# Narrow attentions: products with values in a bank of their own, in pieces, and turned tiles in three banks

## The reference

```python
q = (queries @ q_w + q_b)            # 16 heads of width 16
k, v = (keys @ k_w + k_b), (keys @ v_w + v_b)
scores = einsum('bhqd,bhkd->bhqk', q, k) * scale   # masked
attn = softmax(scores)
out = einsum('bhqk,bhkd->bqhd', attn, v) @ out_w + out_b
```

## Time and profile before

| | |
|---|---|
| median of 3 runs | 1073.18 us (1072.58 to 1073.34) |
| the profiled execution's own time | 1071.5 us |
| its span, first to last instruction | 1069.7 us |
| mean granted TensorE clock | 0.947 of full speed |
| busy: PE, DVE, ACT, POOL | 945.1, 777.2, 606.4, 312.2 us |
| loop of L0a, 32 heads | from 45 to about 162 us |
| loop of L2a | from 831 to about 911 us |
| loop of L3a | from 945 to about 1024 us |

### The profile page before, as it was taken

The page is one execution under the profiler, slowest core; times in us unless marked ns, Lnnn a source line. Parts: engine busy times, 40 slices in busy tenths (PEclk is TensorE's granted clock), DMA queues, the critical chain, the costliest instruction groups (busy, mean ns, idle before and its releaser), DMA issues. The chain is left out here.

```text
span 1069.7 us, 17955 instructions
## 1 busy us (share of the span) xinstructions
PE 945.1 (88%) x6616; PEld 802.0 (75%) x6616; DVE 777.2 (73%) x1621; ACT 606.4 (57%) x1375; POOL 312.2 (29%) x321
## 2 busy tenths in 40 slices
PE   4789886889999999999799999999596898779958
PEld 4666665778999999998689989898475566656647
DVE  3486766468878888886688988878664688668864
ACT  3587883236565555554455655456534688267842
POOL 3454550050221222221121132200004456445510
PEclk8899997989999999999999999999888699889989
DMA  4996004140110111110210111000206820394020
GB/s 144 266 238 103 2 1 185 67 164 1 41 40 1 40 41 40 41 40 2 79 41 3 39 40 41 1 1 2 78 7 159 208 46 2 101 245 67 1 85 21
DMA packets 39506, 72.71 MB, mean 68 GB/s; under 512 B 6550, under 2 KB 23960, under 8 KB 37244
## 3 DMA queue, kind: packets, MB, share of 16 engines
q1 hardware_dynamic: 39420, 71.56, 25.0%
HBM read 55.28 MB, written 16.27 MB: 67 GB/s over the span
## 5 line engine op out<-in xcount | busy, mean ns | idle before, releaser
L1356 ACT CAST L1a_probsT_hi<-L1a_bank 128x512 fp32r<-128x512 f32 x128 | 69.0, 589 | 85.0 <-PE L1a_bank L1232 84.9
L1180 POOL TENSOR_SCALAR L1a_wo_hi<-L1a_stage 128x512 fp32r<-128x512 f32 x16 | 10.4, 652 | 347.5 <-PE L1a_sums L74 339.7
L1391 ACT ACTIVATE L1a_probs<-L1a_scores,L1a_neg_max 128x512 f32<-128x512 f32 x128 | 86.9, 684 | 33.7 <-DVE L1a_bias_shifted L1516 29.2
L1512 DVE TENSOR_REDUCE L1a_top<-L1a_scores 128x2 f32<-128x1024 f32 x64 | 78.2, 1223 | 18.1 <-PE L1a_scores L74 18.1
L72 PE MATMUL L1a_bank<-L1a_probsT_hi,L1a_v_hi 128*128 128x256 f32 x256 | 73.5, 287 | 10.4 <-DVE L1a_probsT_lo L1427 10.4
L1427 DVE TENSOR_TENSOR L1a_probsT_lo<-L1a_bank,L1a_probsT_hi 128x512 fp32r<-128x512 f32 x128 | 82.0, 682 | 0.1
L1358 ACT ACTIVATE L1a_attended_hi<-L1a_bank,L1a_cols 128x256 fp32r<-128x256 f32 x64 | 30.5, 477 | 83.7 <-PE L1a_bank L74 83.5
L72 PE MATMUL L1a_bank<-L1a_w_hi,ctxT_hi 128*128 128x256 f32 x256 | 74.8, 292 | 0.0
L417 POOL TENSOR_SCALAR L0a_probs<-L0a_probs,L0a_inverse 128x768 f32<-128x768 f32 x64 | 57.2, 906 | 58.7 <-DVE L0a_inverse L686 58.7
L74 PE MATMUL L1a_bank<-L1a_probsT_hi,L1a_v_lo 128*128 128x256 f32 x256 | 72.8, 284 | 0.0
L73 PE MATMUL L1a_bank<-L1a_probsT_lo,L1a_v_hi 128*128 128x256 f32 x256 | 72.8, 284 | 0.0
(11 more groups left out here) (422 smaller groups left out, 3089.1 us busy)
## 6 DMA issues: line engine op xcount, KB each, us to landing
L1a_stage<-in_L_w SPq DMA_DIRECT2D x15, 1024.0 KB, 4.8
L0m_fold_wq<-in_L_wqT SPq DMA_DIRECT2D x2, 2048.0 KB, 12.9
L0a_k_dram<-L0a_kT_hi SPq DMA_DIRECT2D x8, 384.0 KB, 10.6
L0a_k_stack<-L0a_k_dram SPq DMA_DIRECT2D x4, 576.0 KB
L0a_w_qkv<-L0a_k_dram SPq DMA_DIRECT2D x4, 576.0 KB
L0a_wide_wo<-in_L_wo SPq DMA_DIRECT2D x1, 2048.0 KB, 17.3
L0a_wide_wo<-in_L_wo SPq DMA_DIRECT2D x2, 1024.0 KB, 18.2
L0m_stage<-in_L_wm SPq DMA_DIRECT2D x4, 512.0 KB, 6.1
```

The costliest lines, as they stand in the source:

```text
L1356: nc.scalar.copy(out, source).then_inc(ring.hi_done, 1)
L1391: nc.scalar.activation(probs[:, g % 2, qt, :], scores[:, qt, :], ACT.Exp, bias=neg_max[:, g % 2, qt:qt + 1], accum_out=row_sum[:, g % 2, q ...
L1512: link(nc.vector.tensor_reduce(top[:, :], scores[:, :, :], AX.X, ALU.max))
```

## The change

The ring loses a bank: one of the four is taken out of it and holds the products with values of all units, one after the other, with semaphores of its own (`values_full`, `values_high`, `values_done`). The turned tiles rotate in the three that are left, and so do all other jobs. A product is cut along the keys into PIECES (3 with 512 keys, with 1, 1 and 2 of the 4 key tiles; 2 with 768 keys, with 3 of the 6 key tiles each), and piece i of unit u stands ahead of the turn of t = 4u + 5 + i. `high_v` and `low_v` come in the step of the last piece, and on ACT and DVE behind that step's copies. On ACT the copy of the first turned bank (c = 0) moves between the two exponentials of a step. The first piece of a unit waits for `low_v` of the unit before, and so does the last unit's product, which is in one. The bias values become two jobs, behind the turns of t = 14 and 15. The turned probabilities get 4 + PIECES slots in place of 5.

```diff
-        TSLOTS = 5
+        PIECES = 3 if nk == S else 2
+        TSLOTS = 4 + PIECES
...
+        values_bank = banks.pop()
         ring = ph.ring(banks)
+        values_full, values_high, values_done = ph.sem("values_full"), ph.sem("values_high"), ph.sem("values_done")
...
-        def product_before(t):
-            return t // 4 - 1 if t % 4 == 1 and t >= 4 else None
-        BIAS_UNIT = 2
+        def piece_beside(t):
+            return divmod(t - 5, 4) if t >= 5 and (t - 5) % 4 < PIECES else None
+        def last_piece(t):
+            return piece_beside(t) is not None and piece_beside(t)[1] == PIECES - 1
+        def bias_beside(t):
+            return t - 14 if cfg["bias_values"] and t in (14, 15) else None
+        values = values_bank[:, 0:Q]
...
-            def product_v(unit):
-                job = job_of["V", unit, 0]
-                ring.wait_bank(pe, job)
+            def product_v(unit, first=0, end=PIECES):
                 b, quad = divmod(unit, quads)
-                for back in range(ring.n):
-                    ring.wait_evacuated(pe, unit_copies(unit)[-1 - back])
-                for kt in range(nkt):
+                if first == 0:
+                    if unit:
+                        pe.wait_ge(values_done, unit)
+                    for back in range(ring.n):
+                        ring.wait_evacuated(pe, unit_copies(unit)[-1 - back])
+                for kt in range(first * nkt // PIECES, end * nkt // PIECES):
...
-                last.then_inc(ring.full, 1)
+                if end == PIECES:
+                    last.then_inc(values_full, 1)
...
                 if t >= 0:
-                    if product_before(t) is not None:
-                        product_v(product_before(t))
-                        if cfg["bias_values"] and product_before(t) == BIAS_UNIT:
-                            values_of_bias()
+                    if piece_beside(t) is not None:
+                        unit, piece = piece_beside(t)
+                        product_v(unit, piece, piece + 1)
                     transpose_head(t)
+                    if bias_beside(t) is not None:
+                        values_of_bias(bias_beside(t))
...
+            def copy_turned(t, c):
+                job = job_of["T", t, c]
+                act.wait_ge(ring.full, job + 1)
+                nc.scalar.copy(probsT[:, t % TSLOTS, c * 512:(c + 1) * 512],
+                               ring.bank(job)[:, :]).then_inc(ring.freed_by(job), 1)
+
             def evacuate(t):
-                if product_before(t) is not None:
-                    high_v(product_before(t))
...
-                for c in range(tj):
+                for c in range(1, tj):
                     if by_act(t, c):
+                        copy_turned(t, c)
+                if last_piece(t):
+                    high_v(piece_beside(t)[0])
...
             for g in range(HEADS + LAG):
                 if g < HEADS:
                     for m in (2 * g, 2 * g + 1):
+                        if m % 2 and g >= LAG:
+                            copy_turned(g - LAG, 0)
                         small = m % small_slots
                         act.wait_ge(max_done, m + 1)
...
+                elif g >= LAG:
+                    copy_turned(g - LAG, 0)
                 if g >= LAG:
                     evacuate(g - LAG)
...
                 if t >= 0:
-                    if product_before(t) is not None:
-                        low_v(product_before(t))
                     for c in range(tj):
                         if not by_act(t, c):
...
+                    if last_piece(t):
+                        low_v(piece_beside(t)[0])
```

More of the change, by code:

```diff
@@ L452, in _, with values_of_bias @@
                 last.then_inc(ring.full, 1)
-            def values_of_bias():
-                job = job_of["B", 0, 0]
+            def values_of_bias(i):
+                job = job_of["B", i, 0]
                 pe.wait_ge(spread_ready, 1)
@@ L458, in values_of_bias @@
                 ring.wait_bank(pe, job)
[L459 to L464, removed]
+                for c in range(4):
+                    for j in range(4):
+                        h = 4 * j + c
+                        last = nc.tensor.matmul(ring.bank(job)[32 * j:32 * j + 32, 0:D], spread[:, i, h, :],
+                                                wide_wo(i * H + h), start=c == 0, stop=c == 3)
                 last.then_inc(ring.full, 1)
@@ L487, in product_v @@
                         moving = probsT[:, g % TSLOTS, :].rearrange("p (t k n) -> p t k n", t=2, k=nkt)[:, :, kt, :]
-                        last = nc.tensor.matmul(ring.bank(job)[32 * j:32 * j + 32, 0:Q],
+                        last = nc.tensor.matmul(values[32 * j:32 * j + 32, :],
                                                 v[:, b * nkt + kt, 32 * (4 * quad + j):32 * (4 * quad + j) + 32],
                                                 moving, start=kt == 0, stop=kt == nkt - 1)
-                last.then_inc(ring.full, 1)
+                if end == PIECES:
+                    last.then_inc(values_full, 1)
             for g in range(HEADS + LAG):
@@ L520, in _ @@
                 if t == 0:
-                    ring.wait_evacuated(pe, job_of["V", own, 0])
+                    pe.wait_ge(values_done, own + 1)
                 if t == 2:
-                    ring.wait_evacuated(pe, job_of["V", own - 1, 0])
+                    pe.wait_ge(values_done, own)
                 ring.wait_bank(pe, job)
@@ L570, in _ @@
                 last.then_inc(ring.freed_by(job), 1)
-            def evacuate(t):
-                if product_before(t) is not None:
-                    high_v(product_before(t))
[L576 to L580, removed]
-                for c in range(tj):
-                    if by_act(t, c):
[L583 to L587, removed]
+            def copy_turned(t, c):
[3 more added lines that the diff above has]
+                               ring.bank(job)[:, :]).then_inc(ring.freed_by(job), 1)
+            def evacuate(t):
+                for c in range(1, tj):
+                    if by_act(t, c):
+                        copy_turned(t, c)
+                if last_piece(t):
+                    high_v(piece_beside(t)[0])
+                if bias_beside(t) is not None:
+                    job = job_of["B", bias_beside(t), 0]
+                    act.wait_ge(ring.full, job + 1)
+                    nc.scalar.copy(keep["bias_values"][:, bias_beside(t), :], ring.bank(job)[:, 0:D]).then_inc(ring.freed_by(job), 1)
             def high_v(unit):
@@ L591, in high_v @@
                     act.wait_ge(mask_written, 16)
-                job = job_of["V", unit, 0]
                 b, quad = divmod(unit, quads)
-                act.wait_ge(ring.full, job + 1)
-                nc.scalar.activation(attended[0][:, quad, b * Q:(b + 1) * Q], ring.bank(job)[:, 0:Q], ACT.Identity,
-                                     bias=bias[:, 4 + quad:5 + quad]).then_inc(ring.hi_done, 1)
+                act.wait_ge(values_full, unit + 1)
+                nc.scalar.activation(attended[0][:, quad, b * Q:(b + 1) * Q], values, ACT.Identity,
+                                     bias=bias[:, 4 + quad:5 + quad]).then_inc(values_high, 1)
             for g in range(HEADS + LAG):
@@ L663, in low_v @@
                 b, quad = divmod(unit, quads)
-                low(job_of["V", unit, 0], v0 + unit, [t[:, quad, b * Q:(b + 1) * Q] for t in attended], 4 + quad, Q)
+                dve.wait_ge(values_high, unit + 1)
+                hi, lo = (t[:, quad, b * Q:(b + 1) * Q] for t in attended)
+                nc.vector.scalar_tensor_tensor(lo, values, bias[:, 4 + quad:5 + quad], raw(hi),
+                                               ALU.add, ALU.subtract).then_inc(values_done, 1)
             for g in range(HEADS + LAG):
```

9 lines of the change are left out of this document (3 added, 6 removed).

## The result

The changed kernel takes 1084.49 us (median of 4 runs, 1080.69 to 1087.75) against 1073.26: a ratio of 1.0116 [1.009, 1.0143], slower. The forecast was 1084.5. The total came out to a tenth of a us, but two groups of its terms are off by 3 to 4 us in opposite directions, as the experiments show, and the runs of the changed kernel spread over 7 us; so that the total is this close is luck. The profiled run is the slowest (1087.75, span 1085.9).

What follows compares the result with a forecast made beforehand. Engines waiting for each other in turn were taken to bound the narrow loops; 11.0 (L0a's chain) - 1.5 (bias values) + 1.8 (L2a and L3a) = +11.3 us on the median 1073.2 gave 1084.5, range 1075.5 to 1094.

Steps and rivals of the forecast that it cites:

- The ring through the copy, L0a: L0a: the copy between exponentials closes a one-step chain through scores, piece and turn; units 15.70 against 13.86, +11.0 us.
- forecast of 9.5: L0a's whole loss: 11.0 us for the closed chain less 1.5 for the bias values.
- Bias values: L0a: one exposed job of 3.64 us becomes two of 1.85 behind turns; -1.5 us (0 to -3.6).
- the second is paid but for 0.3 or so: L0a: of the second bias job's 1.85 us, all but about 0.3 stays exposed.
- rival C: L0a: PE's clock falls to half, pieces and turns about 4 us more a unit, 1112 us; 6 in 100.
- L2a and L3a, steady units: L2a and L3a: the step of the last piece takes 3.46 against 3.56; -0.6 us over six units in each.
- The handover: L2a, L3a: DVE's wait for the high part, then ACT's for the next maximum, is moved by one copy, not removed.
- The sign that I named for it: L2a and L3a: DVE still waits seven times for the high part, about 1.2 us each.
- The end of L2a and L3a: L2a, L3a: the last product now waits for copy, high part and low part; +0.9 us each (0 to 2).
- The first unit: L2a, L3a: pieces at the lower clock after a DMA wait; +0.6 us each (-2 to +2).
- Three banks: L2a and projections: losing one ring bank costs nothing, unless PE's lead runs out; upper bound 10 us an attention.
- PE loses lead and no more: L2a: a turn's second bank waits for the previous turn's first copy, moved forward 0.68; PE, a step ahead, loses nothing.

Runs made afterwards that it cites:

- e3: The changed kernel with the first copy on ACT behind both exponentials again; 1081.47 us, ratio 1.0083.
- e1: The changed kernel with the new form in L0a only, L2a and L3a as in the kernel before; 1085.14 us, ratio 1.0123.
- e4: The changed kernel with L0a's product whole in place of two pieces, ACT's new order kept; 1090.08 us, ratio 1.0161.
- e2: The changed kernel with the new form in L2a and L3a only, L0a as in the kernel before; 1070.65 us, ratio 0.9981.
- e11: The kernel before (four banks, whole product in the ring) with L2a's and L3a's high and low parts a step later; 1105.73 us, ratio 1.0326.
- e5: The kernel before with three banks in place of four for the narrow attentions' ring, nothing else; 1073.29 us, ratio 1.0023.
- e9: e6 with two pieces in all three attentions; 1065.78 us, ratio 0.9949.
- e7: e6 with the first copy between the exponentials in L2a and L3a; 1070.45 us, ratio 0.9988.
- e10: e7 with two pieces in all three attentions; 1057.89 us, ratio 0.9883.
- e6: e3 with the high and low parts of a product taken one step later; 1069.05 us, ratio 0.9978.
- e8: e7 with the old function for L0a; 1074.28 us, ratio 1.0023.

## Why the prediction was right, and where only its sum was

**The ring through the copy, L0a: right.** Each link was within 0.02 (second scores 1.05 for 1.04, product 0.54 for 0.55, piece 1.43 for 1.42, copy 0.70, exponential 0.48 for 0.47), the unit 15.76 for 15.70, and e3 shows the cause by taking it away.

**What else L0a paid.** e1 shows it without L2a and L3a. Six units from 62.06 to 161.06 us take 99.00 us; the same six took 86.33 before (60.94 to 147.27): +12.7 for a forecast of 9.5. (The spans of these two profiles differ by more, 15.3 us: 0.7 stand before the loop, 0.4 in its first steps, 1.0 from the last unit to L2a and 0.5 in L2a, none of them traced. The medians differ by 12.5, so that these six units and the medians agree is in part chance.) The missing 3.2 are:

- Bias values, 1.0. The two units with a bias job exceed a plain one by 0.5 and 2.4, 2.9 in all, where the one job before exceeded it by 3.46. Saved are 0.5, for a forecast of 1.5 (bounds 0 to 3.6). The step that failed is "the second is paid but for 0.3 or so": it is paid whole, 1.93, and PE waits 0.98 for a bank ahead of it, whose copy stands between the exponentials. The row in the profile after:

```profile
112.22 1.93 PE L471 MATMUL L0a_bank<-L0a_wide_wo,L0a_spread 128*32 128x256 f32 x32 [0.98 <-ACT L0a_probsT L587]
```

- The lower clock, 0.9: rival C in part. I gave it 6 in 100, as a fall in every unit. It came in single stretches. In e1 the sixth unit, with a window of 0.72 in it (145 to 151 us), takes 16.68 for 15.77. In the profile after there are two within the six units (96 to 102 and 145 to 150 us), and one behind them (165 to 170); there the six take 99.98. The first bias unit, 17.25 after and 16.30 in e1, where this stretch has 1.00, gives the same price, 0.95.
- The ring, 0.4: 15.76 for 15.70, six times.
- The unit of the first product, 0.9: it takes 16.3 in e1 and after with the clock at 1.00 in the latter (61 to 77 us), and took 13.56. Before, it was 0.3 shorter than its neighbours. Now 0.5 more than in a later unit stands in its first step (62.06 to 65.27, 3.21 for 2.71), where PE's weight loads for the turns wait 0.59 and 0.20 us for POOL; that this wait is the cause was not shown.

The rule of the Trainium skill, "TensorE: Matmul & The Clock Gate", section "A second HAM failure mode: psum-queue depth-cycling", which has the clock swing between its levels when PE is idle briefly and often between groups of matmuls, is borne out in kind: inside L0a's loop, from 60 us to its last exponential, the clock falls in after, e1, e3 (76 to 82 us, copies behind) and e4, and in no other kernel. By that rule it was to be 1112; most units kept the higher level (128 to 146 at 1.00).

**L2a and L3a, steady units: right.** 9.01 for 9.12 is -0.11 a unit, -0.66 in six, forecast -0.6. The handover moved and stayed. The sign that I named for it, about 1.2 us of DVE's wait each time, was off: it is 0.6, since DVE's copy waits for the turn first.

**The end of L2a and L3a: right.** In L2a it was 7.81 from the last head's first exponential to the last high part (903.62 to 911.43) and is 8.75 (916.18 to 924.93): +0.94 for +0.9, and the same in L3a.

**The first unit: wrong sign, the larger error.** I had +0.6 each. Its price before was the lower clock after the wait for a DMA. In e2's L2a, PE's rows at the same place:

```profile
843.12 0.66 PE L482 MATMUL L2a_bank<-ident,L2a_probs 128*128 128x128 f32 x4 [0.42 <-ACT L2a_probsT L587]
...
844.97 0.66 PE L482 MATMUL L2a_bank<-ident,L2a_probs 128*128 128x128 f32 x4 [0.23 <-ACT L2a_probsT L587]
846.89 0.73 PE L516 MATMUL L2a_scores<-L2a_w_qkv,L2a_q_stack 128*128 128x512 f32 x2 [1.27 <-DMA L2a_q_stack<-L2a_q_dram]
847.55 0.64 PE L498 MATMUL L2a_bank<-L2a_probsT,L2a_v 128*32 128x256 f32 x8
```

PE waits 1.27 us for the DMA in place of 2.50, the clock stays (scores 0.73 for 1.22), and the four steps around it (from the sixth head's first exponential to the tenth's) take 8.77 in place of 13.41; in the profile after it is 9.06 in L2a and, with a DMA wait of 3.09 and the clock down for a piece and a turn, 11.96 in L3a. Not all of this is gain, because the step with the parts, 1.6 longer than the others, now stands behind these four. Over the whole loop, from the first exponential to the last head's, e2 has 69.50 for 72.16 in L2a and 69.33 for 70.77 in L3a; less the -0.66 of the steady units, its first units are worth -2.0 and -0.8 for a forecast of +0.6 each. With +0.94 for each end this gives -2.2, and the medians say -2.0. PE's rows in L3a of the profile after, where the clock fell:

```profile
976.40 0.77 PE L516 MATMUL L3a_scores<-L3a_w_qkv,L3a_q_stack 128*128 128x512 f32 x2 [3.09 <-DMA L3a_q_stack<-L3a_q_dram]
977.10 1.08 PE L498 MATMUL L3a_bank<-L3a_probsT,L3a_v 128*32 128x256 f32 x8
```

With three banks some of PE's idle time stands ahead of the turns (0.42 and 0.23) and the rest is shorter. What goes with the clock is the wait for the DMA. There are 28 such waits, two in each of the 14 kernels. In the 5 us behind it the clock is 1.00 in all ten that are 0.59 to 1.56 us long; of the five from 1.70 to 1.95 it fell in two; and behind the thirteen from 2.22 to 3.62 it is 0.50 to 0.67 each time. The clock fell in 5 of 6 with four banks (before, e1 and e11; e11's L2a, with a wait of 1.29, kept it) and in 10 of 22 with three. That the three banks are what shortens the wait is argued and not shown: with them the four steps took 8.8 to 14.1 us, and in the two with the old loops (before and e1) 12.9 to 13.4.

**Three banks: "nothing" was right for this kernel only.** e5 puts them at 0.3 a unit with the copies behind, and e3's 512-key units are 0.5 longer than those of the changed kernel, which does not pay because it also moved the first copy forward. In the 512-key loops the copy's place thus pays for the bank, while in L0a, with two slots of scores, it is what closes the ring. I had seen the first half ("PE loses lead and no more") and not that it hung on the copy. In the changed kernel's L0a the bank shows once, in the 0.98 of the second bias job.

**Left open.** The clock's falls are not settled: the same gaps of 1.33 and 0.75 us stand in units with and without a fall. Why runs of one kernel spread over 7 us (after) and 12 (e9) was not looked into by more profiles of the same kernel; falls of the clock that come in some executions and not in others are a candidate, not a finding.

## What to carry to other kernels

Before moving an evacuation ahead of another instruction on an in-order engine, go round the ring: if that instruction frees the slot that the producer of the evacuated bank has to fill first, the move closes a chain of one step, and its length is a sum of rows that can be had beforehand. A handover between two engines is not removed by giving it another place in the same step; it goes when its result is due a whole step later, and then its buffer must be free that long (e7 and e11 lose all of it to the buffer, e10 gets 0.65 a unit). Where two halves of a change run in loops of different depth, cost and run them apart: the same place of a copy was worth -0.5 us a unit in one loop and +1.6 in the other (e3).

## What the runs showed of the hardware

The granted clock of TensorE fell to 0.70 to 0.75 over windows of 5 to 6 us (each a mean over its two levels: 148 to 151 us of after show 0.51, the 1.2 GHz level) inside a loop with no wait for a DMA, after gaps of 1.33 and 0.75 us that leave it at 1.00 in the next units; each fall cost about 0.9 us in L0a where it could be told (e1, after). After a wait for a DMA of 1.27 or 1.95 us (e2, L2a and L3a) the next scores took 0.73 and the clock held, after 2.50 they took 1.22; after 3.09 (after, L3a) the scores still took 0.77, and the piece behind them 1.08 in place of 0.64. Over the 28 such waits every one up to 1.56 us left the clock up and every one from 2.22 us was followed by a fall, at once or by the turn behind the scores; in between the length of the wait alone does not say it (1.74 in e6 and 1.82 in e4 fell, 1.89 in e8 and 1.95 in e2 held).
